# Attention in a fused two-layer block: mask products by 64 rows, sums of the exponentials on GpSimd alone, and the division in four pieces

## The reference, cut to what matters

```python
q = (x @ Wq).reshape(b, s, 16, 64)      # b = 1, s = 2048 here
k = (x @ Wk).reshape(b, s, 16, 64)
v = (x @ Wv).reshape(b, s, 16, 64)
dot = jnp.einsum('bihd,bkhd->bhik', q, k)
w = jax.nn.softmax(dot / jnp.sqrt(64.), axis=-1)
a = jnp.einsum('bhij,bjhd->bihd', w, v)
return a.reshape(b, s, 1024) @ Wo + bo
```

## Time and profile before

| what | value |
|---|---|
| three runs, median | 1979.29 us (1974.09 to 1983.97) |
| the profiled execution | 1982.01 us |
| its span, first to last instruction | 1980.3 us |
| PE busy | 1745.4 us, 88% |
| DVE busy | 1392.0 us, 70% |
| POOL busy | 1095.0 us, 55% |
| ACT busy | 792.9 us, 40% |

### The profile page before, as it was taken

One profiled execution on the slowest core, in us unless ns is written; L12 is line 12 of the kernel. 1 busy time (PEld: TensorE's weight loads), 2 busy tenths in 40 slices (PEclk: granted clock), 3 DMA queues, 4 the chain that ended last, 5 costly groups with the idle time before them and its releaser, 6 DMA issues.

```text
span 1980.3 us, 35242 instructions
## 1 busy us (share of the span) xinstructions
PE 1745.4 (88%) x13630; PEld 948.8 (48%) x13630; DVE 1392.0 (70%) x2440; ACT 792.9 (40%) x1181; POOL 1095.0 (55%) x644
## 2 busy tenths in 40 slices
PE   4888751948999999999999999999999999995893
PEld 3666641834444444444444444444444444443482
DVE  3666654347787777887777877778778887786474
ACT  3444420533444444444444444444444444441131
POOL 2232204032777677776767767777677777682303
PEclk8886755969999999999999999999999999996897
DMA  7000000210000000000000000000000000003122
GB/s 243 4 3 3 3 1 30 62 38 1 1 1 1 1 1 1 1 1 1 1 1 1 1 1 1 1 1 1 1 1 1 1 1 1 1 1 99 32 58 60
DMA packets 41533, 32.76 MB, mean 17 GB/s; under 512 B 3604, under 2 KB 37392, under 8 KB 41368
## 3 DMA queue, kind: packets, MB, share of 16 engines
q1 hardware_dynamic: 31096, 22.12, 3.6%
q0 software_dynamic: 2048, 4.20, 0.7%
q10 hardware_dynamic: 8224, 4.19, 0.7%
HBM read 18.96 MB, written 11.53 MB: 15 GB/s over the span
## 4 chain that ended last, share of the span: by engine, by line
PE 81%; DVE 9%; issue 5%; POOL 3%; ACT 1%; DMA 1%; SPq 0%; DVEq 0%; POOLq 0%; ACTq 0%
PE psum L1781 23%; PE psum L1766 20%; PE psum L1740 8%; PE psum L1760 6%; PE psum L1407 2%; PE psum L1796 2%; PE psum L1790 2%; PE psum L1181 1%; PE psum L1713 1%; PE psum L1193 1%; PE psum L1367 1%; DVE a_mx L1945 1%; POOL a_acc L2077 1%; PE psum L1417 1%; PE psum L447 1%
## 5 line engine op out<-in xcount | busy, mean ns | idle before, releaser
L2077 POOL TENSOR_TENSOR a_acc<-a_acc,a_Pb 128x832 f32<-128x832 f32 x448 | 893.3, 1994 | 307.8 <-ACT a_Pb L1883 275.1
L1945 DVE TENSOR_REDUCE a_mx<-psum 128x2 f32<-128x1024 f32 x512 | 625.5, 1224 | 237.2 <-PE psum L1740 234.2
L1883 ACT ACTIVATE a_Pb<-psum 128x1024 f32<-128x1024 f32 x512 | 496.7, 1022 | 703.5 <-PE psum L1766 701.5
L1781 PE MATMUL psum<-a_Pb,a_Vb 128*64 128x512 f32 x2048 | 494.3, 604 | 0.0
L1996 DVE TENSOR_TENSOR a_acc<-a_acc,a_Pb 128x192 f32<-128x192 f32 x448 | 230.9, 515 | 28.9 <-ACT a_Pb L1883 5.4
L1781 PEld LDWEIGHTS psum<-a_Pb,a_Vb 128*64 128x64 f32 x2048 | 127.2, 136 | 244.7 <-issue 173.7
L1740 PE MATMUL psum<-a_Kh,a_Qh 64*128 64x512 f32 x1024 | 231.3, 447 | 8.4 <-DVE a_mx L1945 8.3
L1766 PE MATMUL psum<-a_Qh,a_Kh 64*128 64x512 f32 x1024 | 231.1, 447 | 0.0
L1766 PE MATMUL psum<-a_Ql,a_Kh 64*128 64x512 f32 x1024 | 203.8, 393 | 0.0
L1740 PEld LDWEIGHTS psum<-a_Kh,a_Qh 64*128 64x128 f32 x1024 | 97.1, 184 | 222.6 <-issue 211.6
L1766 PE MATMUL psum<-a_Qh,a_Kl 64*128 64x512 f32 x1024 | 203.4, 392 | 0.0
(11 more groups left out here) (385 smaller groups left out, 2004.0 us busy)
## 6 DMA issues: line engine op xcount, KB each, us to landing
x_rows<-zero ACTq DMA_DIRECT2D x2, 2048.0 KB, 20.9
g_w<-in_L_ffn_w_eDF_dram SPq DMA_DIRECT2D x2, 1408.0 KB, 8.7
r_W<-in_L_ffn_W_dram SPq DMA_DIRECT2D x1, 2048.0 KB, 12.4
r_tile_x<-x_rows SPq DMA_DIRECT2D x16, 128.0 KB, 2.1
y_rows<-r_tile_y SPq DMA_DIRECT2D x16, 128.0 KB, 1.8
g_tile_x<-x_rows SPq DMA_DIRECT2D x16, 128.0 KB, 2.2
y_rows<-g_tile_y SPq DMA_DIRECT2D x16, 128.0 KB, 1.8
g_w<-in_L_ffn_w_eFD_dram SPq DMA_DIRECT2D x2, 512.0 KB, 10.5
```

The source lines that it names most:

```text
L1781: last = pe.matmul(ps[HEAD[h], B_O, :], b.Vb[:, p // 2 % 2, kc, at], b.Pb[:, step % BUFS, h * QT:(h + 1) * QT], start=(kc == 0), stop=(kc ...
L1883: act.activation(b.Pb[:, step % BUFS, :], ps[:, slot:slot + 2, :].rearrange("p a b -> p (a b)"), ACT.Exp, scale=SCALE).then_inc(S["probs"], 1)
L1945: v.tensor_reduce(b.mx[:, :, qc, quarter:quarter + 1], ps[:, bank:bank + 2, :], AX.X, ALU.max).then_inc(S[f"free{bank}"], 1)
L2077: g.tensor_tensor(b.acc[:, u, at], before, b.Pb[:, step % BUFS, at], ALU.add).then_inc(S["added_pool"], 1)
```

## The change

The first part makes the mask product like the scores: for each step two products of 64 rows, each directly ahead of the step's own score products, where four of 32 rows stood ahead of both steps. The negated maxima are then written once for each head and not twice. The second step's product waits for the second exponential of the round before, and the first one for the first alone.

The second part gives GpSimd all 1024 columns of `acc`. VectorE's `add` is gone.

The third part cuts `normalise` into four pieces of 128 columns, at d = 3, 5, 6 and 7; the sums and the output projection change places (d = 1 and d = 2), and the four `invert` come one round earlier (d = 2 to 5) and ahead of the early reduction. TensorE's projection waits for all four pieces, as before for the one.

```diff
-    if d == 1 and U > 1:
+    if d == 1 and U:
+        return "sum", U - 1
+    if d == 2 and U > 1:
         return "out", U - 2
-    if d == 2 and U:
-        return "sum", U - 1
...
-        if R:
-            pe.wait_ge(S["probs"], 2 * R)
-        for g in range(4):
-            rows = slice(32 * g, 32 * (g + 1))
-            pe.matmul(ps[:, 2 * (g % 2) + g // 2, :], b.ones[rows, :], b.Mr[rows, :], start=True, stop=False, tile_position=(32 * g, 0))
         for i in range(2):
             kc, slot = 2 * d + i, 2 * i
             at = slice(kc * P, (kc + 1) * P)
+            if R:
+                pe.wait_ge(S["probs"], 2 * R - 1 + i)
+            for h in range(2):
+                pe.matmul(ps[:, slot + h, :], b.ones[HEAD[h], :], b.Mr[HEAD[h], :], start=True, stop=False)
...
-    def normalise(U):
-        v.wait_ge(S["inverted"], 4 * U + 4)
+    def normalise(U, part):
+        v.wait_ge(S["inverted"], 4 * U + part + 1)
         v.wait_ge(S["heads_out"], U + 1)
...
-        v.tensor_tensor(b.On[:, :], b.rec[:, :], b.Or[:, U % 2, :], ALU.mult).then_inc(S["normalised"], 1)
+        at = slice(part * P, (part + 1) * P)
+        v.tensor_tensor(b.On[:, at], b.rec[:, at], b.Or[:, U % 2, at], ALU.mult).then_inc(S["normalised"], 1)
...
-        if R:
-            if (R - 1) % RN:
-                add(2 * R - 2)
-            add(2 * R - 1)
+        if U and 2 <= d <= 5:
+            invert(U - 1, d - 2)
         if early:
             maximum(*early[1:])
...
-        if U and 3 <= d <= 6:
-            invert(U - 1, d - 3)
-        if U and d == 7:
-            normalise(U - 1)
+        if U and d in (3, 5, 6, 7):
+            normalise(U - 1, (3, 5, 6, 7).index(d))
...
-        u, at = U % 2, slice(0, POOL)
+        u = U % 2
...
-        before = b.Pb[:, (step - 1) % BUFS, at] if kc == 1 else b.acc[:, u, at]
-        g.tensor_tensor(b.acc[:, u, at], before, b.Pb[:, step % BUFS, at], ALU.add).then_inc(S["added_pool"], 1)
+        before = b.Pb[:, (step - 1) % BUFS, :] if kc == 1 else b.acc[:, u, :]
+        g.tensor_tensor(b.acc[:, u, :], before, b.Pb[:, step % BUFS, :], ALU.add).then_inc(S["added"], 1)
```

More of the change, by code:

```diff
@@ L1561 @@
 STEPS = 2 * ROUNDS
-POOL = 832
 BUFS = 8
@@ L1785, in sums @@
     def sums(U):
-        pe.wait_ge(S["added_dve"], 15 * (U + 1))
-        pe.wait_ge(S["added_pool"], 15 * (U + 1))
+        pe.wait_ge(S["added"], 15 * (U + 1))
         bank = begin(("sum", U))
@@ L1793, in output @@
     def output(U):
-        pe.wait_ge(S["normalised"], U + 1)
+        pe.wait_ge(S["normalised"], 4 * U + 4)
         bank = begin(("out", U))
@@ L1880, in probs @@
             act.wait_ge(S["weighted"], step - BUFS + 1)
-            act.wait_ge(S["added_dve"], adds_of(step - BUFS))
-            act.wait_ge(S["added_pool"], adds_of(step - BUFS))
+            act.wait_ge(S["added"], adds_of(step - BUFS))
         act.activation(b.Pb[:, step % BUFS, :], ps[:, slot:slot + 2, :].rearrange("p a b -> p (a b)"), ACT.Exp, scale=SCALE).then_inc(S["probs"], 1)
@@ L1887, in heads_out @@
         if U > 1:
-            act.wait_ge(S["normalised"], U - 1)
+            act.wait_ge(S["normalised"], 4 * U - 4)
         act.activation(b.Or[:, U % 2, :], ps[:, B_O, :], ACT.Copy).then_inc(S["heads_out"], 1)
@@ L1944, in maximum @@
         bank = begin(("max", U, m))
+        if U and m == 0:
+            v.wait_ge(S["negated"], U)
         v.tensor_reduce(b.mx[:, :, qc, quarter:quarter + 1], ps[:, bank:bank + 2, :], AX.X, ALU.max).then_inc(S[f"free{bank}"], 1)
@@ L1953, in negate @@
             v.wait_ge(S[f"full{bank}"], n)
[L1954 to L1957, removed]
+        nm = b.nm[:, :].rearrange("p (h x) -> p h x", h=2)[:, :, 0:4]
+        v.tensor_reduce(nm, b.mx[:, :, :, :], AX.X, ALU.max, negate=True).then_inc(S["negated"], 1)
     def mask(U):
@@ L1964, in invert @@
     def invert(U, part):
+        if U and part == 0:
+            v.wait_ge(S["normalised"], 4 * U)
         bank, n = plan.at["sum", U]
@@ L1968, in invert @@
         v.reciprocal(b.rec[:, at], b.ssum[:, at]).then_inc(S["inverted"], 1)
-    def normalise(U):
-        v.wait_ge(S["inverted"], 4 * U + 4)
+    def normalise(U, part):
+        v.wait_ge(S["inverted"], 4 * U + part + 1)
         v.wait_ge(S["heads_out"], U + 1)
-        if U:
+        if U and part == 0:
             bank, n = plan.at["out", U - 1]
             v.wait_ge(S[f"full{bank}"], n)
-        v.tensor_tensor(b.On[:, :], b.rec[:, :], b.Or[:, U % 2, :], ALU.mult).then_inc(S["normalised"], 1)
+        at = slice(part * P, (part + 1) * P)
+        v.tensor_tensor(b.On[:, at], b.rec[:, at], b.Or[:, U % 2, at], ALU.mult).then_inc(S["normalised"], 1)
     def output(U):
@@ L1984, in output @@
         v.tensor_tensor(yq, ps[:, bank, :].rearrange("p (a d) -> p a d", a=4), yq, ALU.add).then_inc(S[f"free{bank}"], 1)
[L1986 to L1994, removed]
-        before = b.Pb[:, (step - 1) % BUFS, at] if kc == 1 else b.acc[:, u, at]
-        v.tensor_tensor(b.acc[:, u, at], before, b.Pb[:, step % BUFS, at], ALU.add).then_inc(S["added_dve"], 1)
     v.wait_ge(S["tile_y0"], 16 * (SLOTS_T // 2))
@@ L2002, in attention_dve @@
     dve.wait()
-    for g in range(4):
-        rows = slice(32 * g, 32 * (g + 1))
-        dve.did(v.tensor_copy(b.mask[rows, :, :], bcast(k.ident[rows, 32 * g:32 * g + 4].unsqueeze(2), [32, 4, P])))
+    for h in range(2):
+        dve.did(v.tensor_copy(b.mask[h * D:h * D + 32, :, :], bcast(k.ident[h * D:h * D + 32, h * D:h * D + 4].unsqueeze(2), [32, 4, P])))
     gather_norm_dve(k, 0, k.y_all, k.x_all, 1)
@@ L2039, in attention_dve @@
             {"q": queries, "k": keys, "mask": mask, "out": output}[key[0]](*key[1:])
-        if U and 3 <= d <= 6:
-            invert(U - 1, d - 3)
-        if U and d == 7:
-            normalise(U - 1)
-    for step in (STEPS - 2, STEPS - 1):
-        add(step)
+        if U and d in (3, 5, 6, 7):
+            normalise(U - 1, (3, 5, 6, 7).index(d))
     output(UNITS - 2)
@@ L2048, in attention_dve @@
         invert(UNITS - 1, part)
-    normalise(UNITS - 1)
+        normalise(UNITS - 1, part)
     output(UNITS - 1)
@@ L2074, in add @@
         if step > 1:
-            g.wait_ge(S["added_pool"], adds_of(step - 1) if kc > 1 else 15 * U)
-        before = b.Pb[:, (step - 1) % BUFS, at] if kc == 1 else b.acc[:, u, at]
-        g.tensor_tensor(b.acc[:, u, at], before, b.Pb[:, step % BUFS, at], ALU.add).then_inc(S["added_pool"], 1)
+            g.wait_ge(S["added"], adds_of(step - 1) if kc > 1 else 15 * U)
+        before = b.Pb[:, (step - 1) % BUFS, :] if kc == 1 else b.acc[:, u, :]
+        g.tensor_tensor(b.acc[:, u, :], before, b.Pb[:, step % BUFS, :], ALU.add).then_inc(S["added"], 1)
     for step in range(STEPS):
```

## The result

The changed kernel takes 1964.48 us by median (1959.85 to 1968.33, 7 runs) against 1982.16 (1973.49 to 1985.16, 7 runs) for the kernel before: 0.9918, with a 95% interval of 0.9895 to 0.9941. It is 0.8% faster. The forecast was 1962, faster. The profiled execution took 1963.51 us.

What follows compares the result with a forecast made beforehand. A round costs what TensorE's queue costs. From 1982: 40 off for mask products, 18 on for collisions, 4 on at the end, 5 off for accidents, 3 on for a new one: 1962 us; 8 in 10 range 1941 to 1985.

Steps and rivals of the forecast that it cites:

- The mask products: TensorE's queue: fewer height changes save 0.16 us a round (bounds 0.15 and 0.18) in 247 rounds, 40 us off.
- GpSimd's addition: 1024 columns take 2.35 us, pitch 2.47; GpSimd keeps up except in rounds d = 5 and 6, without a gap there.
- The collisions: Division pieces wait for GpSimd's addition, delaying reductions after the late product's start T; d = 5 free; 18 us on.
- What stands behind a late product: Early products start 0.39 us late at d = 7, 0.13 at next d = 0; with late-loading weights about 0.52 a unit.
- The end: Last unit: GpSimd's fifteen longer additions 3 us on, the four pieces between the last inversions 1 on.
- The accidents: Two slow units, where a VectorE addition waited for GpSimd and the clock then fell to 0.50, go: 5 us off.
- A reading that was wrong: VectorE's 30 additions a unit at 0.358 free 11 us less the wait, hidden under TensorE's time and worth nothing.
- the 3 for new accidents: New collisions may end in an accident of their own; 3 us added for one.
- GpSimd's pace at 2.42: Rival: GpSimd's addition takes 2.42 by proportion, so collisions cost 33 us in all, 1978 us; chance 0.17.
- no collisions: Rival: pauses shift GpSimd's phase so the pieces fall between its additions, 1941 us; chance 0.15.
- The rival by the clock: Rival: TensorE's pauses bring stretches at clock 0.50, 3 us each, in one unit of three or all, 1993 to 2055; chance 0.14.
- the signs named: Mask pair 0.34 behind late product, jobless round 4.41, additions 2.35, unit 40.8 to 41.0, reduction waits 12 to 20 us.

Runs made afterwards that it cites:

- e8: e3 with the old mask products by 32 rows, so also without the division: 1983.94 us, 1.0013 of the kernel before.
- e3: Changed kernel without the division: projection reads undivided heads, each piece is a one-column, one-input VectorE instruction: 1938.49 us, 0.9763 of the kernel before.
- e6: e5 with the last unit's additions on VectorE, all 1024 columns, none on GpSimd: 1936.54 us, 0.9778 of the kernel before.
- e7: Changed kernel with only the last unit's additions moved to VectorE, none on GpSimd: 1954.35 us, 0.9860 of the kernel before.
- e1: Kernel before with only the mask products by 64 rows, VectorE's additions kept: 2000.96 us, 1.0076 of the kernel before.
- e5: Changed kernel with division pieces right behind the late reduction at d = 3 to 6, inversions behind the early one: 1942.79 us, 0.9810 of the kernel before.
- e10: e6 with the pieces of d = 5 and 6 as one of 256 columns at d = 5: 1935.28 us, 0.9768 of the kernel before.
- e4: Changed kernel with the division in one instruction of 512 columns at d = 7: 1977.79 us, 0.9959 of the kernel before.
- e2: Changed kernel with the old mask products, 32 rows in front of both steps: 1999.94 us, 1.0091 of the kernel before.

## Why the prediction was right

It was right in direction, place and size. From the execution that it was worked out from, 20 us were forecast (1982 to 1962) and 18.5 measured (1982.0 to 1963.5); between medians 17.7 were measured. By its steps:

- **The mask products** were forecast at 0.16 us a round, 40 us. The mechanism is shown by e8 against e3, and the size is 0.19 a round, 45 us. The term that was mis-sized is the pairs' 0.24. The late pair's 0.34 was right (0.35 in the trace after), but the pairs behind it take 0.24 and then 0.23 each, so the upper bound (pairs at 0.23, 0.18) was nearer.
- **GpSimd's addition**: 2.35 forecast, 2.376 by median, and 0.144 between two of them where 0.12 was taken. It keeps up in d = 1 to 4 and runs without a wait in d = 5 to 7, as worked out.
- **The collisions**: d = 5 free, d = 6 and d = 7 late, as worked out. The reduction of d = 7 was forecast at T + 1.14 and starts at T + 1.30. Two things make the 0.16. The addition that the piece of d = 6 waits for, GpSimd's third from d = 5 on, ends 0.11 later than forecast, since it is 2.52 from start to start and not 2.47. And the late product of d = 7 comes 0.06 earlier, since the rounds d = 5 and 6 take 4.36 and 4.40 and not 4.41 each.
- **What stands behind a late product**: the early products were forecast 0.39 and 0.13 late at d = 7 and d = 0, with 0.1 in each for weights that load late. The trace has 2.67 - 2.21 = 0.46 and 2.32 - 2.21 = 0.11 at their starts, and the 0.1 comes on top, behind them: L1746 follows at 1081.52, 0.42 after the early product, where the trace before has 0.33 between the same two (1007.47 and 1007.80), and L1712 follows 0.43 after its one, where e3 has 0.33. For L1746 the negation that it waits for could be the reason too; L1712 waits for nothing of VectorE's. In all that is 0.77, and e3 says 0.78, against 0.52 forecast. In the 31 units it is 25.5 us and not 18: 18.0 in the first 24 (12.5 forecast) and 7.5 in the last seven (5.6).
- **The end**: 3 + 1 forecast; the part behind the last writing of `Mr` grew by 6.6. TensorE's wait for the last addition grew by 7.47 - 1.95 = 5.5, where I had taken the middle between 0 and 5.8 because the unit's first rounds would hide part. They could not: GpSimd comes into the last unit already behind. Its first addition there starts 7.5 us after the last writing of `Mr` (1734.69), and 5.0 us in the kernel before (1756.83). The four pieces between the inversions are worth the 1 forecast: from the sums to the projection 7.6 us pass, and 6.8 before. e6 and e7 place the wait in GpSimd's additions.
- **The accidents** of the kernel before were put at 5 us, and are gone. Before and e8, which has the same mask products and no two-input instruction in the rounds, differ by 6.1 in the 31 units, all of it in the two units around the pause of 1.38 and the last two, around that of 1.80. The low clock behind them is gone as well: every unit of the changed kernel behind the first reads 1.00. That fits the cause given (an addition that waits for GpSimd); e1, which keeps the additions, has 51 pauses at the reductions.
- **A reading that was wrong and costs nothing**: VectorE has 15 additions in a unit and not 30 (the earlier trace rows has x448 for 32 units, which is 14, and one more adds the unit's first two exponentials), so the freed time is 5.4 us a unit and not 11. It lies under TensorE's either way.

The terms as measured are -45.3 + 25.5 + 6.6 - 6.1, and 1.2 ahead of the first unit, where nothing was changed. Together that is -18.1, against 1980.3 - 1962.3 = 18.0 between the spans. The forecast was -40 + 18 + 4 - 5 + 3. The mask products gave 5 more than forecast and the collisions cost 7.5 more, and the 3 for new accidents, none of which came, nearly made up for the end. The mechanism was right; that the sum came within 2 us is in part luck.

The rivals: GpSimd's pace at 2.42 did not come about; no collisions did not either, though e5 and e10 show that it was to be had. The rival by the clock has its own run: e4 brings pauses of up to 1.4 us in nearly every unit, every unit behind the first reads 1.00, and it costs only the pauses. Of the signs named, the waits for reductions came out a little under the 12 to 20 us (11.7 from 470 to 1785).

What the prediction did not say, and e1 and e2 do: neither half is a gain without the other. Shorter rounds with the additions kept make 51 pauses of up to 1.6 us out of 2. The removal without shorter rounds pays for the pieces and for the later end with nothing; without the pieces it is level with the kernel before (e8, 1.0013).

## What to carry to other kernels

When the engine that sets the time gets a shorter queue, look next at who must be ready sooner: a wait that was hidden in a round of 4.57 us shows in one of 4.40. In these traces a VectorE instruction with two SBUF inputs that starts while GpSimd adds lasts until about 0.15 us (pieces of 128 columns) or 0.2 us (additions of 192) behind the end of GpSimd's instruction. So it belongs where little is left of GpSimd's instruction and where nothing urgent is queued behind it. Inversions, with one input (0.953 at most), and the writing of `Mr`, with one input in PSUM (0.680 to 0.693), do not show such waits and can fill the other places. The Trainium skill's rule of the exclusive lock (SBUF — State Buffer, two separate sides: whichever of the two starts first has the shared port pair for its whole instruction) holds here with 1.34 to 1.99 us for pieces of 0.29.

## What the runs showed of the hardware that was not expected

A pause of TensorE alone does not bring the lower clock. In the kernel before, a pause of 1.38 us was followed by 3.3 us at a granted clock of 0.50, the 1.2 GHz level. e1 pauses for 1.56 in the timeline above, and e4 for 0.97 in the unit looked at (up to 1.4 elsewhere). The stretches just behind these two pauses, e1 first:

```profile
1097.90:1101.50 3.60, 3.56 (x26) 2.72 (x28) 3.29 (x6) 1.95 (x2) 1.63 (x2) 1.00 0.00 0
```

```profile
1092.00:1096.00 4.00, 3.92 (x19) 1.81 (x21) 2.09 (x3) 1.37 (x3) 3.40 (x2) 1.00 0.00 0
```

Both are at 1.00, the 2.4 GHz level. So is every unit of e1 and of e4 behind the first, over all their pauses, while in the kernel before the two units in which the clock fell, behind pauses of 1.38 and 1.80, read 0.96. What else decides, no run here shows.
